# Starting the moving operands of the gate products 32 bytes past a multiple of 64

## The chip, the cores and the metric

The kernel runs on one core of a Trainium2 chip. The metric is the device time of one execution in microseconds (us): the median of three runs before the change is 1782.2 us (1781.26 to 1783.71). The engines are TensorE (PE; its loads of stationary operands are listed apart, as PEld), VectorE (DVE), ScalarE (ACT), GpSimd (POOL) and SyncE (SP), which issues nearly all DMAs. A matmul on PE takes a stationary operand, loaded first by its own LDWEIGHTS instruction, and a moving operand, which streams past it. Both are read from on-chip memory, where a tensor starts at the same byte address in each of 128 partitions. This document is about that address modulo 64.

## What is computed

64 graphs of 256 nodes with 256 features pass through two layers, each with a residual:

```
# layer 0
h = relu(layernorm(x));  x = x + relu(norm_adj @ h @ W.T + b)
# layer 1
h = relu(layernorm(x))
x_conv = relu(bn(conv17(relu(bn(conv1(h))))) + h)        # "branch"
A      = exp(-dist(h)) * adj;  msg = relu(h @ w_msg.T + b_msg)
x_nmp  = A @ msg                                        # "messages"
gi = concat(x_conv, x_nmp) @ w_ih.T + b_ih              # 512 -> 768
gh = h @ w_hh.T + b_hh                                  # 256 -> 768
r, z = sigmoid(gi_r + gh_r), sigmoid(gi_z + gh_z)
n = tanh(gi_n + r * gh_n)
x = x + (1 - z) * n + z * h
```

## The kernel before

**Products in three parts.** Most products are done on fp32r operands. Each fp32 tensor is split into a rounded high part and the remainder (names ending in h and l), and `mm3` (L99) yields for each block of 128 input features three matmuls: high by high, high by low, low by high. `multiply` (L109) issues them, so that all have line L111 in the profile, and are told apart by their operands: the profile writes `P<-moving,stationary` in no fixed order.

**Three stages.** The first (turns of one graph each) does layer 0 and the front of layer 1. Each turn has, on PE and in this order, 12 matmuls of 256 columns for layer 0 (`w0` moving, `ag` stationary), 12 of 256 columns for the messages (`ax` moving, `ms` stationary), 8 records of plain fp32 matmuls (`ah` moving, `hd` stationary), 2 for distances, 6 of 256 columns for the small projection (`xx` moving, `wse` stationary), 8 for a Fourier transform, 12 of 512 columns (`w1m` moving, `xx` stationary) and 4 transposes. The second stage multiplies spectra by filters, one frequency after another (`wh` moving, `xh` stationary, 256 columns). The third computes the gates, for 32 pairs of graphs, two output halves each.

**The third stage.** `gate` (L1056) takes its stationary operands from `wg` (128 columns of the weights w_ih and w_hh) and its moving operands from three tensors: `xcx` (branch, blocks 0 and 1), `nmx` (messages, blocks 2 and 3) and `xnx` (normalized input, blocks 4 and 5). Each is a high and a low tensor of 2 x 512 values per partition, and there are two of each for alternate pairs. A pair needs 18 blocks in each of two output halves, so 2 x 18 x 3 = 108 matmuls of 512 columns. In the very last half-pair the last 18 matmuls are split in two halves of 256 columns. Between the two halves of a pair 40 small matmuls of the inverse transform stand (`gt` moving, `yt` stationary, L1016). ACT writes the high parts (L979, L991, L1050), POOL and DVE the low parts (L986, L998, L1039). ACT and DVE evaluate the gates from PSUM, and DVE transposes and adds the result.

**Order of the work.** Each engine has its own program, written out by hand, and they wait for each other on semaphores. Nothing of the order depends on addresses.

**Addresses.** A `Place` (L72) hands out addresses in sequence and rounds each tensor's size up to a multiple of 32 bytes. `keep` starts at a multiple of 64 (L151). Which tensors start at 32 modulo 64 follows from the sizes (bytes per partition):

- `cold` (96 bytes) brings `gt` and `tt_w` to 32; `tt_w` (2268, rounded to 2272) brings all that follows back to 0.
- In the first stage `half`, `guard` (32 each) and `s2t` (148, rounded to 160) bring `sm`, `ag`, `xn`, `xt` and `xx` to 32 (L183 to L188); L190 starts again at a multiple of 64.
- `w0`, `w1m`, `wse`, `hd`, `ah`, `ax`, `ms`, `wh`, `xh`, `xsum`, `wsum` and `wg` start at 0.
- `xnx`, `nmx` and `xcx`, the third stage's moving operands, start at 0.

All these offsets within a tensor (blocks of 128, 256 or 512 values) are multiples of 64 bytes, so an operand has the same remainder as its tensor.

| matmuls | moving starts at | stationary starts at | columns |
|---|---|---|---|
| `w0`, `ag` (layer 0) | 0 | 32 | 256 |
| `ax`, `ms` (messages) | 0 | 0 | 256 |
| `xx`, `wse` (small projection) | 32 | 0 | 256 |
| `w1m`, `xx` (conv1 and msg) | 0 | 32 | 512 |
| `wh`, `xh` (frequencies) | 0 | 0 | 256 |
| gates | 0 | 0 | 512 |

Of the kernel before, what the change touches and what calls it, by code (L numbers as in the profile page):

```python
# [126 lines left out]
def gnn_kernel(nc, x, adj, adjt, w0t, w1mt, wset, wgt, w2r, bc, cols, ftab, gtab, ttab, eye, out):  # L127
# [19 lines left out]
    with ExitStack() as ctx:  # L147
# [13 lines left out]
        third = Place(nc, keep.at)  # L161
# [3 lines left out]
        third = Place(nc, keep.at)  # L165
        wf = [keep("wf0", [128, 20, 2, 256])]
        raw_wg = [third(f"st_wg{c}", [128, 768]) for c in range(6)]
        xnf = [third(f"xnf{i}", [128, 2, 2, 256]) for i in range(2)]
        nms = [third(f"nms{i}", [128, 2, 256]) for i in range(2)]
        xnx = [third.hl("xnx0", [128, 2, 512])]  # L170

        p1, p2, p3 = Place(nc, keep.at), Place(nc, keep.at), Place(nc, keep.at)
# [54 lines left out]
        mt = [p2(f"mt{i}", [128, 256]) for i in range(2)]  # L227
        yo = [p2(f"yo{i}", [128, 512]) for i in range(4)]

        xnx.append(p3.hl("xnx1", [128, 2, 512]))  # L230
        yt = [p3(f"yt{i}", [128, 5, 128]) for i in range(4)]
        nmx = [p3.hl(f"nmx{i}", [128, 2, 512]) for i in range(2)]
        xct = [p3(f"xct{i}", [128, 2, 256]) for i in range(2)]
        xcx = [p3.hl(f"xcx{i}", [128, 2, 2, 256]) for i in range(2)]
        oo = [p3(f"oo{i}", [128, 2, 2, 256]) for i in range(2)]
        tr = p3("tr", [128, 512])
        tz = p3("tz", [128, 512])
# [1316 lines left out]
```

## Time and profile before

| | |
|---|---|
| median of three runs | 1782.2 us |
| profiled execution, first to last instruction | 1779.4 us |
| PE busy | 1765.8 us, 99% |
| PEld, DVE, ACT, POOL busy | 87%, 68%, 56%, 47% |
| TensorE matmuls | 10778 |
| first stage | to about 655 us |
| second stage | to about 900 us |
| third stage | the rest, about 875 us |

No device time of the profiled execution is given apart from its span, 1779.4 us, which stands 2.8 us under the median of the runs. "Busy" of PE is the sum of the intervals in which at least one matmul is recorded; since a matmul of 512 columns is recorded with 390 ns and the next one starts some 227 ns later, the busy time and the mean duration do not tell the rate. The rate is read from the starts in the timeline: the difference of two starts by the number of matmuls between them.

### The profile page before, as it was taken

To read this page: it belongs to the slowest core of one execution; us is meant where nothing else is said; L and a number is where in the kernel's file an instruction comes from. 1 tells how busy PE (TensorE), PEld (TensorE's weight loads), DVE (VectorE), ACT (ScalarE), POOL (GpSimd) and SP (SyncE) were. 2 spreads that over 40 slices of the span, in tenths; PEclk is the share of its full clock that TensorE was granted. 3 is DMA by queue.
4 is the path that set the end of the run, shared out by engine and by line. 5 is a ranking of instruction groups with operands and counts; after the bars stand their busy time and mean duration, and the time that the engine had idled before them with its cause. 6 is when DMAs were issued, how large, how long until landed. Compare 5 with 4: busy or idle time off the path is not lost.

```text
span 1779.4 us, 30974 instructions
## 1 busy us (share of the span) xinstructions
PE 1765.8 (99%) x10778; PEld 1556.5 (87%) x10778; DVE 1211.7 (68%) x2318; ACT 1001.1 (56%) x1787; POOL 830.1 (47%) x988
## 2 busy tenths in 40 slices
PE   8999999999999999999999999999999999999998
PEld 7999999999999999999988888888888888888887
DVE  8999999999999946555664554554544545545545
ACT  6888888888888866656643233332333332333322
POOL 5788888887777627665722221221221222212211
PEclk9999999999999999999999999999999999999999
DMA  7566667666656464544663434435445344344342
GB/s 224 174 206 208 209 204 209 203 207 196 207 182 205 141 176 145 176 161 173 234 188 96 102 95 116 94 97 120 86 102 125 79 108 106 92 115 95 98 111 42
DMA packets 531865, 262.70 MB, mean 148 GB/s; under 512 B 366215, under 2 KB 494471, under 8 KB 531710
## 3 DMA queue, kind: packets, MB, share of 16 engines
q1 hardware_dynamic: 531166, 260.66, 52.5%
q8 instruction: 87, 1.43, 0.3%
q14 instruction: 68, 0.56, 0.1%
q10 hardware_dynamic: 544, 0.07, 0.0%
HBM read 151.58 MB, written 109.05 MB: 146 GB/s over the span
## 4 chain that ended last, share of the span: by engine, by line
PE 96%; DVE 1%; issue 1%; POOL 1%; ACT 0%; DMA 0%; DVEq 0%; POOLq 0%; ACTq 0%
PE P L111 72%; PE P L612 6%; PE P L1016 4%; PE P L871 4%; PE P L641 4%; PE P L703 4%; PE P L660 1%; PE P L621 1%; POOL axl L575 0%; POOL af L572 0%; DVE sm L483 0%; DVE sm L489 0%; DMA x<-in_x 0%; DVE agl L417 0%; DVE x L470 0%
## 5 line engine op out<-in xcount | busy, mean ns | idle before, releaser
L998 POOL TENSOR_TENSOR xnx1l<-xnf,xnx1h 128x1024 fp32r<-128x1024 f32 x16 | 43.9, 2744 | 343.7 <-ACT xnx1h L991 343.7
L998 POOL TENSOR_TENSOR xnx0l<-xnf,xnx0h 128x1024 fp32r<-128x1024 f32 x15 | 41.5, 2768 | 311.5 <-ACT xnx0h L991 311.5
L1117 ACT ACTIVATE tr<-P,cold 128x512 f32<-128x512 f32 x64 | 44.2, 690 | 213.1 <-PE P L111 213.1
L1120 ACT ACTIVATE nn<-gn,col 128x512 f32<-128x512 f32 x64 | 46.4, 724 | 183.0 <-DVE gn L1141 183.0
L1137 DVE SCALAR_TENSOR_TENSOR gn<-tr,gn 128x512 f32<-128x512 f32 x64 | 45.4, 709 | 138.8 <-ACT tr L1117 138.8
L572 POOL TENSOR_TENSOR af<-af,at 128x512 f32<-128x512 f32 x64 | 110.4, 1725 | 42.2 <-ACT af L363 40.3
L575 POOL TENSOR_TENSOR axl<-af,axh 128x512 fp32r<-128x512 f32 x64 | 101.3, 1582 | 55.6 <-ACT axh L381 55.6
L1150 DVE SCALAR_TENSOR_TENSOR tz<-tz,tr 128x512 f32<-128x512 f32 x63 | 43.6, 692 | 119.4 <-ACT tz L1131 119.4
L612 PE MATMUL P<-ah,hd 128*128 128x256 f32 x512 | 121.7, 381 | 0.3 <-ACT hd L397 0.3
L1131 ACT ACTIVATE tz<-P,cold 128x512 f32<-128x512 f32 x63 | 43.4, 688 | 133.7 <-PE P L111 133.7
L111 PE MATMUL P<-w1mh,xxh 128*128 128x512 f32 x256 | 107.8, 421 | 0.0
L1141 DVE TENSOR_TENSOR gn<-gn,P 128x512 f32<-128x512 f32 x64 | 44.0, 688 | 88.2 <-PE P L111 88.1
L612 PEld LDWEIGHTS P<-ah,hd 128*128 128x128 f32 x512 | 93.2, 191 | 10.7 <-ACT hd L397 0.5
L111 PE MATMUL P<-w1mh,xxl 128*128 128x512 f32 x256 | 101.3, 396 | 0.0
L111 PE MATMUL P<-w1ml,xxh 128*128 128x512 f32 x256 | 101.0, 395 | 0.0
L495 DVE SCALAR_TENSOR_TENSOR x<-x,x 128x512 f32<-128x512 f32 x64 | 99.6, 1557 | 0.1
L896 DVE TENSOR_TENSOR yo<-P,mt 128x512 f32<-128x512 f32 x78 | 53.5, 686 | 66.2 <-PE P L111 66.2
L1016 PEld LDWEIGHTS P<-gt,yt 64*128 64x128 f32 x1280 | 76.4, 187 | 11.3 <-issue 11.3
L111 PE MATMUL P<-w0h,agh 128*128 128x256 f32 x256 | 77.1, 301 | 4.3 <-DVE w0l L460 2.1
L1016 PE MATMUL P<-gt,yt 64*128 64x72 f32 (+2 forms) x1280 | 81.0, 278 | 0.0
L703 PE MATMUL P<-tt_w,taps 119*128 119x140 f32 (+1 forms) x592 | 80.8, 282 | 0.0
L723 ACT COPY wf<-P 128x420 f32<-128x420 f32 (+1 forms) x94 | 46.8, 512 | 60.0 <-PE P L703 59.8
(214 smaller groups left out, 6413.2 us busy)
## 6 DMA issues: line engine op xcount, KB each, us to landing
xh_d<-xst SPq DMA_DIRECT2D x64, 320.0 KB, 4.8
y_d<-yo SPq DMA_DIRECT2D x80, 256.0 KB, 2.1
yt<-y_d SPq DMA_DIRECT2D x128, 160.0 KB, 3.9
xl<-xh_d SPq DMA_DIRECT2D x36, 512.0 KB, 4.6
x<-in_x SPq DMA_DIRECT2D x64, 256.0 KB, 2.7
a<-in_adj SPq DMA_DIRECT2D x64, 256.0 KB, 3.0
at<-in_adjt SPq DMA_DIRECT2D x64, 256.0 KB, 4.1
x_d<-x SPq DMA_DIRECT2D x64, 256.0 KB, 4.4
```

The source lines that it names most:

```text
L111: done = e.matmul(o, l, r, start=start, stop=stop, skip_group_check=True)
L495: e.e.scalar_tensor_tensor(out=o[:, :, :], in0=o[:, :, :], scalar=0.0, in1=xs[b % 5][:, :, :], op0=ALU.max, op1=ALU.add).then_inc(S["x2"], 1)
L572: e.e.tensor_tensor(af[:, :], af[:, :], at[b % 7][:, :], ALU.mult).then_inc(S["am"], 1)
L575: e.e.tensor_tensor(ax[1][:, :], af[:, :], ax[0][:, :], ALU.subtract).then_inc(S["axlo"], 1)
L612: t = e.e.matmul(P[AG][:, f * 256:f * 256 + 256], hd[b % 2][:, m, f * 128:f * 128 + 128], ah[b % 2][:, m * 256:m * 256 + 256], start=m == ...
L641: t = e.e.matmul(P[k][:, n * 2 * NT:n * 2 * NT + 2 * NT], h1[b % 2][:, n, c * 128:c * 128 + 128], ft[:, :], start=True, stop=True, skip_gr ...
L703: t = e.e.matmul(P[k][:, m * 140:m * 140 + 140], taps[0:n_rows, j0 + m, c * 128:c * 128 + 128], tt_w[0:n_rows, part * 140:part * 140 + 140 ...
L723: e.e.copy(dst, src).then_inc(S["wev"], 1)
L871: t = e.e.matmul(common(chunk)[:, 0:256], xsum[f % 3][:, c, 128 * chunk:128 * chunk + 128], wsum[f % 3][:, c, :], start=c == 0, stop=c == ...
L896: e.e.tensor_tensor(yo[n % 4][:, :].rearrange("p (q o) -> p q o", q=2), main(chunk)[:, :].rearrange("p (q o) -> p q o", q=2), mt[chunk][:, ...
L998: e.e.tensor_tensor(o[1][:, :, :], xnf[p % 2][:, :, :, :].rearrange("p c i t -> p c (i t)"), o[0][:, :, :], ALU.subtract).then_inc(done, 1)
L1016: t = e.e.matmul(P[idft_bank(b, o)][:, first:end], y[rows, q, :], gt[rows, g:g + end - first], start=q == 0, stop=q == 4, skip_group_check ...
```

## The change

Two lines of padding of 32 bytes are put ahead of the moving operands, so that `xnx0`, `xnx1`, `nmx` and `xcx` start at 32 modulo 64. `nmx` and `xcx` now stand next to `xnx1`, and `yt`, `xct` and the rest come behind them, after a third padding that brings them back to 0 modulo 64. `xct`, `yt`, `oo`, `tr`, `tz`, `gn`, `nn`, `ot` and `x2l` have other addresses than before and the same remainder, 0. `wg` stays where it was. No instruction, no wait, no shape and no order on any engine changes.

```diff
@@ -167,6 +167,7 @@
         raw_wg = [third(f"st_wg{c}", [128, 768]) for c in range(6)]
         xnf = [third(f"xnf{i}", [128, 2, 2, 256]) for i in range(2)]
         nms = [third(f"nms{i}", [128, 2, 256]) for i in range(2)]
+        third.at += 32
         xnx = [third.hl("xnx0", [128, 2, 512])]
 
         p1, p2, p3 = Place(nc, keep.at), Place(nc, keep.at), Place(nc, keep.at)
@@ -227,11 +228,13 @@
         mt = [p2(f"mt{i}", [128, 256]) for i in range(2)]
         yo = [p2(f"yo{i}", [128, 512]) for i in range(4)]
 
+        p3.at += 32
         xnx.append(p3.hl("xnx1", [128, 2, 512]))
+        nmx = [p3.hl(f"nmx{i}", [128, 2, 512]) for i in range(2)]
+        xcx = [p3.hl(f"xcx{i}", [128, 2, 2, 256]) for i in range(2)]
+        p3.at += 32
         yt = [p3(f"yt{i}", [128, 5, 128]) for i in range(4)]
-        nmx = [p3.hl(f"nmx{i}", [128, 2, 512]) for i in range(2)]
         xct = [p3(f"xct{i}", [128, 2, 256]) for i in range(2)]
-        xcx = [p3.hl(f"xcx{i}", [128, 2, 2, 256]) for i in range(2)]
         oo = [p3(f"oo{i}", [128, 2, 2, 256]) for i in range(2)]
         tr = p3("tr", [128, 512])
         tz = p3("tz", [128, 512])
```

## Rows read from the trace of the kernel before

**Rows 1.** The page: span, busy time of engines, granted TensorE clock by slice.
```profile
span 1779.4 us, 30974 instructions
...
PE 1765.8 (99%) x10778; PEld 1556.5 (87%) x10778; DVE 1211.7 (68%) x2318; ACT 1001.1 (56%) x1787; POOL 830.1 (47%) x988
...
PEclk9999999999999999999999999999999999999999
```

**Rows 2.** Windows: the third stage; one pair of it. PE, PEld, DVE, ACT, POOL busy.
```profile
905.00:1779.40 874.40, 869.26 (x4753) 723.08 (x4751) 442.08 (x651) 282.71 (x418) 191.10 (x93) 1.00 0.44 101
1302.35:1329.52 27.17, 27.17 (x151) 22.58 (x149) 13.65 (x21) 8.83 (x14) 6.18 (x4) 1.00 0.45 102
```

**Rows 3.** Chain that ended last, in that pair: start us, us, what.
```profile
1302.42 24.70 PE P L111 x108
1327.12 2.46 PE P L1016 x40
```

**Rows 4.** Waits, PE, whole span: us in total, times, longest.
```profile
PE P L111 <- DVE w0l L460: 2.1, 1, 2.1
```

**Rows 5.** Waits, all engines, third stage.
```profile
ACT tr L1117 <- PE P L111: 213.1, 64, 3.4
```

**Rows 6.** Groups of gate matmuls by form: count, busy us, mean ns.
```profile
L111 PE MATMUL P<-xnx0h,wgh 128*128 128x512 f32 x192 | 76.5, 398 | 0.0
...
L111 PE MATMUL P<-xcx1l,wgh 128*128 128x512 f32 x190 | 73.9, 389 | 0.0
...
L111 PE MATMUL P<-xnx1l,wgh 128*128 128x256 f32 x4 | 1.1, 283 | 0.0
```

**Rows 7.** Timeline of PE, gates of one pair: start us, us, what.
```profile
1302.69 0.39 PE L111 MATMUL P<-xnx0l,wgh 128*128 128x512 f32 x1
...
1304.52 0.39 PE L111 MATMUL P<-xnx0h,wgh 128*128 128x512 f32 x1
...
1326.74 0.39 PE L111 MATMUL P<-xcx1h,wgl 128*128 128x512 f32 x1
```

**Rows 8.** Timeline of PE, first stage: conv1 and msg.
```profile
284.95 0.39 PE L111 MATMUL P<-w1ml,xxh 128*128 128x512 f32 x1
...
287.28 0.40 PE L111 MATMUL P<-w1mh,xxl 128*128 128x512 f32 x1
287.52 0.60 PE L660 MATMUL P<-ident,xn 128*128 128x128 f32 x4
```

**Rows 9.** Timeline of PE, same turn: layer 0, messages, fp32, small projection.
```profile
288.07 0.28 PE L111 MATMUL P<-w0l,agh 128*128 128x256 f32 x1
...
289.36 0.28 PE L111 MATMUL P<-axh,msh 128*128 128x256 f32 x1
...
289.71 0.28 PE L111 MATMUL P<-axh,msh 128*128 128x256 f32 x1
...
290.67 0.28 PE L111 MATMUL P<-axh,msl 128*128 128x256 f32 x1
290.79 1.89 PE L612 MATMUL P<-ah,hd 128*128 128x256 f32 x8
292.33 0.59 PE L621 MATMUL P<-uv 96*128 96x256 f32 x2
292.76 0.28 PE L111 MATMUL P<-xxh,wseh 128*128 128x256 f32 x1
...
293.46 1.25 PE L641 MATMUL P<-ft,h 128*128 128x160 f32 x8
```

**Rows 10.** Timeline of PE, last half gates, 256 columns.
```profile
1770.02 0.28 PE L111 MATMUL P<-xnx1h,wgl 128*128 128x256 f32 x1
...
1773.98 0.28 PE L111 MATMUL P<-xcx1h,wgl 128*128 128x256 f32 x1
```

**Rows 11.** ACT casts: tensors at 32 modulo 64; at 0.
```profile
L336 ACT CAST xxh<-xt 128x512 fp32r<-128x512 f32 x64 | 39.7, 620 | 3.8 <-DVE s2t L1391 1.8
L381 ACT CAST axh<-af 128x512 fp32r<-128x512 f32 x64 | 39.7, 620 | 2.6 <-POOL af L572 1.1
```

## The prediction

> **What bounds the kernel now.** I read the page's busy times first: PE is busy 1765.8 of 1779.4 us, and the granted clock is 9 tenths or more in each of the 40 slices, so full speed (2.4 GHz) nearly throughout [rows 1]. The windows then give the third stage, where the change lies: 874.40 us at a clock of 1.00, PE busy 869.26, the next engine, DVE, 442.08 [rows 2]. One pair of graphs takes 27.17 us, in which PE has no gap and DVE is busy 13.65, ACT 8.83, POOL 6.18 [rows 2]. The chain that ended last runs through PE alone there: 24.70 us of gate matmuls, 2.46 of the inverse transform [rows 3]. PE waits for nobody in this stage; its longest wait of the whole run is 2.1 us, at the start [rows 4]. The others wait for PE, as ACT's 213.1 us for the gate r [rows 5]. So in this stage time is the number of matmuls by the distance of their starts, and only that distance counts.
>
> The last view is the timeline, which gives it. In a pair the first matmuls start 228.8 ns apart (1302.69 to 1304.52 over 8), and then the distance settles: 1304.52 to 1326.74 over 98 is 226.7 ns, the same for all three tensors [rows 7]. At 2.4 GHz 512 columns stream in 213.3 ns (512 / 2.4), so each matmul pays 13.4 ns beyond its streaming. The change can only act on this piece, or add to it.
>
> **What the change does, step by step.** No instruction is added or moved, no wait either. Three things change: the remainder of the moving operands (0 to 32), of what ACT, DVE and POOL write when they fill them, and the plain position of some other tensors.
>
> *How many matmuls.* The three tensors times the three products give nine groups for the even pairs, with 192 matmuls of 512 columns each, and nine for the odd pairs, with 190 each: 9 x 192 + 9 x 190 = 3438. The last half-pair adds nine groups of 4 with 256 columns, 36 (the first, the last and a short one of these groups are shown) [rows 6].
>
> *What each costs at other remainders.* No matmul of the trace has 512 columns with the moving operand alone at 32, so I bound it by the nearest rows. The nearest in size is conv1 and msg: 512 columns, moving at 0, stationary at 32. Its starts lie 233.0 ns apart (284.95 to 287.28 over 10), or 233.6 with the step to the transposes (to 287.52 over 11) [rows 8]; I take 233.3. That is 6.6 ns over the gates' 226.7. It is not the busier first stage that makes it slow: messages, both operands at 0, run at 120.0 ns in the same turn (289.71 to 290.67 over 8) [rows 9], and the last half gates, both at 0 in the quiet third stage, at 120.0 ns too (1770.02 to 1773.98 over 33) [rows 10]. So a row with both at 0 runs alike in both stages, and what differs in conv1 is the remainder.
>
> Does a moving operand at 32 act like a stationary one at 32? With 256 columns the trace has both. Layer 0 (stationary at 32): 288.07 to 289.36 over 11, 117.3 ns. Small projection (moving at 32): 292.76 to 293.46 over 6, 116.7 ns. Both at 0: 120.0 [rows 9]. The two mixed cases agree within the rounding of the rows and differ from the equal case by the same 3 ns. I read this as: what counts is whether the two streams have the same remainder. Equal ones settle in a fixed rhythm (226.7, 120.0), unequal ones don't. With 256 columns that is a little faster, since there the load of the stationary operand is nearly as long as the matmul; with 512 it is slower. By this the gates go from 226.7 to 233.3 ns.
>
> *The sum.* 3438 x 6.6 ns = 22.7 us. The first 8 of each pair already stand at 228.8, so they lose 2.1 less: 32 x 8 x 2.1 ns = 0.5 us off. The 36 short ones may gain 36 x 3 ns = 0.1. Net +22.1 us. Made against the profiled span: 1779.4 + 22.1 = 1801.5; the runs' median stands 2.8 over the span, so 1804.3. I forecast 1804 us.
>
> *Bounds of this term.* From above: single steps in conv1, such as 287.28 to 287.52, are 240 ns by the rows [rows 8]; 3438 x 13.3 = +46 us. From below: the plain fp32 matmuls, whose moving operand is used at half the rate, start at most 220 ns apart (290.79 to 292.33 holds at least 7 steps) [rows 9], and nothing excludes that a broken rhythm lets the gates reach it: 3438 x (220 - 226.7) = -23 us. I take the value of the row nearest in columns, which is conv1's.
>
> *The writes.* ACT's cast between tensors at 32 takes 620 ns, and the same cast between tensors at 0 takes 620 ns [rows 11]: nothing on ACT. Were DVE's or POOL's low parts slower, the cover is large: DVE is idle 13.5 of a pair's 27.17 us, and POOL 21 [rows 2]. Cost 0; without that cover it would be a few hundred ns per pair.
>
> *The moved tensors.* `yt`, the stationary operand of the inverse transform, keeps its remainder, as do all of DVE's and ACT's work tensors. Only distances between addresses change; I know of no row in which distance shows. Cost 0, with the 0.2% band as its bound.
>
> *A rule that speaks against this.* The Trainium skill, "TensorE: Matmul & The Clock Gate", section "Part 2: What happens when you issue a matmul", says that PE has two independent read ports and that loading the next stationary operand takes no bandwidth from the running matmul; its section "Back-to-back issue gap" gives N/2.4 + 2.5 ns, 215.8 for 512 columns. The trace doesn't agree: 226.7 with both operands at 0, and 233 in conv1. "SBUF — State Buffer", section "Specifications (TRN2)", names lines of 16 bytes; both 0 and 32 are whole lines, and its section "Operand start alignment" makes address a matter of legality. By these pages the sum would be 0, which is the first rival below.
>
> **The rivals.**
>
> *No effect (1782).* The moving stream's start doesn't matter, and conv1 is slow because its stationary operand begins at 32 (a load that touches one more piece of 64 bytes). For it: conv1's odd side is indeed the stationary one, and the gates' stays at 0. Against it: the small projection, with only the moving side at 32, leaves 120.0 ns just as layer 0 does. The time would be 1782.2.
>
> *Faster.* The fixed rhythm of equal remainders is itself the loss. With unequal ones the load's reads fall between the moving stream's, and each matmul saves what it saves with 256 columns. The place is the start of each gate matmul, the price 120.0 - 117.0 = 3 ns, 3438 x 3 = 10.3 us: 1772. If it reached the fp32 matmuls' 220 ns, 1759. It decides as soon as the step falls under 225.7 ns (3.6 us, 0.2% of the time, by 3438 is 1 ns). Against it: conv1 has unequal remainders at 512 columns and is slower than the gates, and there the saving would have to appear as well.
>
> *Slower by another amount.* The moving stream touches 33 pieces of 64 bytes instead of 32. If it pays just for the two halves, half of conv1's excess or up to double of it are both possible: 3.3 ns, 1793, or 13.3 ns, 1828.
>
> *The change doesn't do what it says.* All sizes ahead of the padding are multiples of 64 but for those listed, so each of the twelve moving tensors does land at 32. I give this no chance of its own.
>
> **Chances.** Conv1's rate, 1804, with its own range 1798 to 1811: 0.52. Slower by another amount: 0.15 (two thirds of it below 1798). No effect: 0.18. Faster: 0.15. The band within which a measurement of this kernel can't tell a change is about 0.2%, 3.6 us. The slower side has 0.67; a little of the no-effect case and of the smallest losses falls across the band's edge, so slower 0.68, same 0.17, faster 0.15. The range that holds the time 8 times in 10 takes in no effect, the half excess and conv1's rate: 1779 to 1813.
>
> **What would show it.** In the timeline of the changed kernel the starts of a pair's gate matmuls would lie 233 ns apart and never settle at 226.7; the pair's period would go from 27.17 to about 27.87 us, the chain's piece of 108 from 24.70 to about 25.4, the third stage from 874.4 to 896.5. The first two stages would stay within 1 us, the 40 matmuls of the inverse transform at 2.46 us, PE without waits in the stage. It would be wrong if the steps stayed at 226.7 (the stationary side alone counts), if they fell below it (the rhythm was the loss), or if the time came from another place, such as a wait of PE on DVE or POOL.

## The result, and the profile after

The changed kernel takes 1803.15 us (median of 4 runs, 1802.9 to 1803.56), the kernel before 1781.73 us beside it. The ratio is 1.012 (95% interval 1.0108 to 1.0132), so it is 21.4 us slower. The forecast was 1804.

The windows of the changed kernel (one pair of graphs, then the third stage; columns as in [rows 2]):

```profile
1312.80:1340.67 27.87, 27.87 (x151) 22.56 (x149) 13.68 (x21) 8.84 (x14) 6.20 (x4) 1.00 0.47 99
905.00:1801.80 896.80, 891.53 (x4756) 722.55 (x4754) 442.70 (x651) 282.89 (x418) 191.41 (x93) 1.00 0.45 98
```

Against [rows 2], the pair went from 27.17 to 27.87 us and the stage from 874.40 to 896.80, with the busy times of DVE, ACT and POOL within 1 us of before, and the same clock. The chain through that pair:

```profile
1310.42 2.46 PE P L1019 x40
1312.89 25.39 PE P L111 x108
```

Against [rows 3], 108 gate matmuls take 25.39 instead of 24.70 us; the 40 of the inverse transform still take 2.46. The timeline of PE in the same pair, 1 and 95 matmuls apart, shows the step:

```profile
1315.72 0.40 PE L111 MATMUL P<-nmx0h,wgh 128*128 128x512 f32 x1
1315.95 0.39 PE L111 MATMUL P<-nmx0l,wgh 128*128 128x512 f32 x1
...
1337.88 0.39 PE L111 MATMUL P<-xcx1h,wgl 128*128 128x512 f32 x1
```

1315.72 to 1337.88 over 95 is 233.3 ns, where [rows 7] have 226.7. The duration of one, 0.39 or 0.40, shows almost nothing of it. The last half gates, 256 columns:

```profile
1792.29 0.28 PE L111 MATMUL P<-xnx1l,wgh 128*128 128x256 f32 x1
...
1796.26 0.28 PE L111 MATMUL P<-xcx1h,wgl 128*128 128x256 f32 x1
```

1792.29 to 1796.26 over 34 is 116.8 ns, where [rows 10] have 120.0: the short matmuls became faster, as the short rows of the first stage had suggested. Who fills the moving operands is not slower; ACT's cast of the normalized input, before and after:

```profile
L991 ACT CAST xnx0h<-xnf 128x1024 fp32r<-128x1024 f32 x16 | 16.6, 1036 | 0.0
```

```profile
L994 ACT CAST xnx0h<-xnf 128x1024 fp32r<-128x1024 f32 x16 | 16.6, 1036 | 0.0
```

### The profile page after: what moved, and what is told of

Its sections match the earlier page's. It is cut to its first block, busy times and chain, and to the rows that moved or that the text cites. A ratio compares the mean times of both kernels' runs of the same rounds, so it can differ in the third digit from the quotient of the medians.

```text
span 1801.8 us, 30974 instructions
## 1 busy us (share of the span) xinstructions
PE 1786.6 (99%) x10778; PEld 1554.7 (86%) x10778; DVE 1212.7 (67%) x2318; ACT 1001.2 (56%) x1787; POOL 830.0 (46%) x988
## 4 chain that ended last, share of the span: by engine, by line
PE 96%; issue 1%; DVE 1%; POOL 1%; DMA 0%; ACT 0%; SPq 0%; DVEq 0%; POOLq 0%; ACTq 0%
PE P L111 73%; PE P L615 6%; PE P L1019 4%; PE P L874 4%; PE P L644 4%; PE P L706 4%; PE P L663 1%; PE P L624 1%; PE P L1478 0%; DMA tt_w<-in_ttab 0%; POOL axl L578 0%; POOL af L575 0%; DVE sm L486 0%; DVE sm L492 0%; DVE x L473 0%
## 5 line engine op out<-in xcount | busy, mean ns | idle before, releaser
L874 PE MATMUL P<-wsum,xsum 128*128 128x256 f32 x312 | 80.2, 378 | 0.0
```

The costliest lines, as they stand in the source:

```text
L874: t = e.e.matmul(common(chunk)[:, 0:256], xsum[f % 3][:, c, 128 * chunk:128 * chunk + 128], wsum[f % 3][:, c, :], start=c == 0, stop=c == ...
```

## The experiments

Theory R, behind the forecast: what counts is whether the two operands of a matmul have the same remainder. Theory M: the moving operand's own start counts. "Distance" below is the start of the moving operand minus that of the stationary one, modulo 256. In each run I read the chain's piece of 108 gate matmuls (24.70 us before, 25.39 after). e1, e2, e3 and e10 were executed 4 to 11 times, the others once each; the kernel before took 1781.03 to 1783.71 us throughout.

**Padding of 64 instead of 32** (e1)

```diff
-        third.at += 32
+        third.at += 64
         xnx = [third.hl("xnx0", [128, 2, 512])]
-        p3.at += 32
+        p3.at += 64
         xnx.append(p3.hl("xnx1", [128, 2, 512]))
...                             # the third padding too: 64 for 32
```

> The changed kernel with paddings of 64 bytes instead of 32: the same new order of the tensors, but the moving operands of the gates start at 0 modulo 64 again. Theory R (what counts is whether the moving and the stationary operand of a matmul have the same remainder modulo 64): the gate matmuls start 226.7 ns apart, time as before, about 1782 us. Theory M (a moving operand must start at a multiple of 64, whatever the stationary one does): the same, 1782. Rival P (the new order or neighbours of the tensors cost, or the remainder that counts is modulo 128): 233.3 ns, about 1803 us.

```profile
1305.78 24.94 PE P L111 x108
```

Ratio to before 1.0043 (1.0028 to 1.0058): 1789.2 us. All starts are multiples of 64, and still 108 matmuls take 0.24 us more, 2.2 ns each. Neither theory had this, and the remainder modulo 64 is not the whole rule. The rival's time (1803) was wrong too, its kind (a longer remainder) right.

**Both operands at 32** (e2) and **the stationary one alone** (e3)

```diff
# e2: on the changed kernel; e3: on the kernel before
+        third.at += 32
         wg = third.hl("wg", [128, 6, 768])
```

> The changed kernel with 32 bytes of padding ahead of wg as well, so that the stationary and the moving operands of the gates both start at 32 modulo 64. Theory R (equal remainders): 226.7 ns from start to start, about 1782 us. Theory M (the moving operand's own start): 233.3 ns, 1803 us. A third, L (each operand that begins off a multiple of 64 costs by itself): more than 233.3 ns, up to 240, 1803 to 1826 us.

> The kernel before with 32 bytes of padding ahead of wg alone: stationary operands of the gates at 32 modulo 64, moving ones at 0, as in conv1 and msg of the first stage. Theory R: 233.3 ns, about 1803 us. Theory M: 226.7 ns, 1782 us, and then conv1's slow rate has another cause. Theory L: 233.3 ns, about 1803 us.

The chain of e2, then of e3:

```profile
1303.36 24.70 PE P L111 x108
```

```profile
1312.61 25.40 PE P L111 x108
```

e2 is at 1781.8 us, ratio 1.0001 (0.9991 to 1.0011); e3 at 1803.2, ratio 1.0121 (1.0106 to 1.0136). This decides between R and M: the change is undone by shifting the stationary operand as well, and done as fully by shifting it alone. Theory L falls with M, since in e2 both operands start off a multiple of 64 and nothing is lost. e2 has the new order of the tensors and all other new addresses, so these cost nothing.

**Only xnx at 32** (e4)

```diff
         xnx.append(p3.hl("xnx1", [128, 2, 512]))
+        p3.at += 32
         nmx = [p3.hl(f"nmx{i}", [128, 2, 512]) for i in range(2)]
         xcx = [p3.hl(f"xcx{i}", [128, 2, 2, 256]) for i in range(2)]
-        p3.at += 32
         yt = [p3(f"yt{i}", [128, 5, 128]) for i in range(4)]
```

> The changed kernel with nmx and xcx at multiples of 64 again, and xnx alone at 32. If the loss is paid matmul by matmul, the 36 of a pair's 108 that read xnx start 233 ns apart and the others settle at 226.7, and the span is about 36/108 of 22.4 = 7.5 us over 1779.4. If one odd group upsets the rhythm of the rest, the others stay at 230 or more, and the span is 15 us or more over.

```profile
1308.36 25.08 PE P L111 x108
```

The span is 1791.8 us, 12.4 over before, between the two expectations, which had overlooked that `nmx` and `xcx` land at a distance of 64 here, not 0. With e1's 2.2 ns for these, 36 x 6.6 + 72 x 2.2 ns = 0.40 us over 24.70; measured 0.38. So the loss is paid matmul by matmul, by each one's own distance, and the payments add up to within 0.02 us.

**Distances of 16 and 144 mixed, 96, 128, 256 and 512** (e5, e6, e7, e12, e13). In e5 each moving tensor is a view that begins 4 values into a tensor 32 values longer, on the kernel before. The 32 values are 128 bytes, so the high tensors, which come first, start at a distance of 16, and the low ones behind them at 144: of 108 matmuls 72 are at 16 and 36 at 144. The others are e1 with another number.

```diff
+    def hl16(self, name, shape):
+        n = math.prod(shape[1:])
+        flat = [self(f"{name}{h}", [128, n + 32], F32R)[:, 4:4 + n] for h in "hl"]
...
-        third.at += 32
+        third.at += 96      # e6; e7: 128, e12: 256, e13: 512; p3.at the same
```

> The kernel before with the moving operands of the gates starting 16 bytes into slightly longer tensors: 16 modulo 128, stationary ones at 0. So far the step from start to start is 226.7 ns at a difference of 0, 229.0 at 64 and 233.3 at 32 (all modulo 128). Theory R in its narrow form (the same 64-byte piece is what counts, each stream a whole number of pieces apart): anything off 0 is as bad as 32, 233 ns, a span of about 1801 us. Rival G (the step depends on the distance in a graded way): between 226.7 and 233.3, a span of 1780 to 1800.

> The changed kernel with paddings of 96 bytes: moving operands at 96 modulo 128, stationary at 0. The run with wg alone moved had the difference -32, the same as 96 modulo 128, and 233.3 ns. Theory R (only the difference counts): 233.3 ns, and the span within 1 us of 1801.6. If the absolute start of the moving operand matters beside the difference: another step, and a span at least 3 us away.

> The changed kernel with paddings of 128 bytes, the control for the run with 64, which lost 7.7 us where neither theory expected a loss. If the remainder modulo 128 is what counts: 226.7 ns, span about 1779.4 us. If the order or the neighbours of the tensors cost: 229 ns as with 64, span about 1787 us. If still larger distances count (256 or 512): something else than 226.7.

> The changed kernel with paddings of 256 bytes. At a distance of 128 between the two operands' remainders the step was 232.7 ns and not the 226.7 that theory R expected, so the remainder modulo 64 is too short a rule. Theory R512 (the moving and the stationary start must agree modulo 512 bytes, the length of one stationary row of 128 values, which is the remainder that all gate operands share in the kernel before and in the run with both at 32): at 256 no fixed step, 229 to 234 ns, a span of 1787 to 1803 us. Theory R256 (agreement modulo 256 is enough): 226.7 ns, a span of 1780 us.

> The changed kernel with paddings of 512 bytes, otherwise as the one with 256. Both R512 and R256: 226.7 ns, span 1779.4 to 1780.5 us. Rival Q (still larger distances count, or the padding itself): 229 to 234 ns, span 1787 to 1803 us.

The chain's piece of one pair in each of the five, in this order, and behind that of e5 four starts in a row:

```profile
1310.03 25.16 PE P L118 x108
...
1311.46 0.40 PE L118 MATMUL P<-xnx0h,wgh 128*128 128x512 f32 x1
1311.70 0.40 PE L118 MATMUL P<-xnx0l,wgh 128*128 128x512 f32 x1
1311.93 0.39 PE L118 MATMUL P<-xnx0h,wgl 128*128 128x512 f32 x1
1312.15 0.40 PE L118 MATMUL P<-xnx0h,wgh 128*128 128x512 f32 x1
```

```profile
1313.07 25.40 PE P L111 x108
```

```profile
1311.48 25.30 PE P L111 x108
```

```profile
1303.35 24.71 PE P L111 x108
```

```profile
1303.38 24.71 PE P L111 x108
```

The last half gates of the same runs give the step of matmuls of 256 columns, from the second start to the 36th. That of e6, as an example:

```profile
1792.58 0.28 PE L111 MATMUL P<-xnx1l,wgh 128*128 128x256 f32 x1
...
1796.66 0.27 PE L111 MATMUL P<-xcx1h,wgl 128*128 128x256 f32 x1
```

| distance | 0 | 16 and 144 (e5) | 32 | 64 | 96 | 128 | 224 (e3) | 256 | 512 |
|---|---|---|---|---|---|---|---|---|---|
| 108 matmuls of 512 columns, us | 24.70 | 25.16 | 25.39 | 24.94 | 25.40 | 25.30 | 25.40 | 24.71 | 24.71 |
| step at 256 columns, ns | 120.0 | 117.9 | 116.8 | 117.6 | 120.0 | 118.5 | 117.9 | 120.0 | 120.0 |

First the row of 512 columns. e5 lies within rival G's range and below the narrow theory's 233 ns, but it shows the mean of two distances: in the rows the step to and from a low tensor is 0.24 and 0.23 us and the one between two high tensors 0.22, again and again. What 16 alone costs is not shown. At 96 the loss is the same as at 224 (e3), as the theory of the difference said, though by a rule modulo 128 that then failed: at 128 the loss is nearly full (every third pair takes 25.40 us, the others 25.29 or 25.30), and at 256 it is gone. R512 was too strict, R256 held: of the distances tried, all multiples of 256 run at the fast step and no other does. Distances of 160 and 192 were not tried at 512 columns.

The row of 256 columns, of 34 steps each, is not the first one turned round. All multiples of 256 are at 120.0 here too, but 96 is as well, although it costs the long matmuls as much as any; 32 gains 3.2 ns and 224, its mirror image, only 2.1.

**Half the load** (e8 on the kernel before, e9 on the changed one)

```diff
-            w = [{c: h[:, c, n * 256 + o * 128:n * 256 + o * 128 + 128] ...
+            w = [{c: h[:, c, n * 256 + o * 128:n * 256 + o * 128 + 64] ...
-            return multiply(e.e, mm3(w, mov, P[k][:, 0:end - at], ...
+            return multiply(e.e, mm3(w, mov, P[k][0:64, 0:end - at], ...
```

> The kernel before, but each gate matmul takes 64 of its 128 stationary columns and writes 64 partitions of its result; the other half of the gates is left out, all other work stays. Moving columns and their number are unchanged. Theory R explains the 13.4 ns that a gate matmul takes beyond the 213.3 ns of its streaming by reads of the stationary operand that collide with the moving stream's: half as many reads, so 6 to 8 ns beyond, a step of 219 to 222 ns, and a span 16 to 26 us below 1779.4. Rival S (the 13.4 ns are a fixed price of starting an fp32r matmul): 226.7 ns, span as before.

> The changed kernel (moving operands of the gates 32 bytes off the stationary ones), with 64 of 128 stationary columns in each gate matmul; half of the gates is left out, all other work stays. With half the load and no distance the short matmuls had gone from 120.0 to 113.3 ns, but the long ones from 226.7 to 229.8, without a fixed rhythm. Theory C (what a matmul takes beyond its streaming are collisions of the two read streams, in proportion to the load): beyond 213.3 ns half of 20, so about 223 ns, and short ones at about 112 ns; a span near 1767 us. Rival W (with a short load no distance settles, and 229 to 230 ns is what any unsettled long stream takes): 229 to 230 ns, a span near 1788 us, the same as at no distance. If the distance costs by itself whatever the load: 233 ns, span 1801.

The chain of e8, and from its timeline two starts of short matmuls:

```profile
1306.50 24.98 PE P L111 x108
```

```profile
1778.98 0.28 PE L111 MATMUL P<-xnx1h,wgl 128*64 128x256 f32 x1
...
1782.72 0.28 PE L111 MATMUL P<-xcx1h,wgl 128*64 128x256 f32 x1
```

The same of e9:

```profile
1308.74 25.08 PE P L111 x108
```

```profile
1782.90 0.28 PE L111 MATMUL P<-xnx1h,wgh 128*64 128x256 f32 x1
...
1786.71 0.28 PE L111 MATMUL P<-xcx1h,wgl 128*64 128x256 f32 x1
```

With half the load and distance 0 the short matmuls fall from 120.0 to 113.3 ns (3.74 us over 33): what they take beyond 106.7 ns halves (106.7 ns is what 256 more columns add at distance 0, 226.7 - 120.0, and so an estimate of the streaming of 256). But the long ones get slower, 24.98 instead of 24.70 us. At distance 32 the long ones gain (25.08 instead of 25.39) and the short ones, from 1782.90 over 32 steps, are at 119.1 ns, slower than with the full load. A fixed price per matmul (rival S) is out, and so is a price in proportion to the load (theory C). The edit also halves the partitions of the result that a matmul writes, so by itself it doesn't say that the load is what counts; that the stationary operand's address counts is shown by e3. Of rival W half came: its step was nearly right, about 230 ns in e8 and 231 in e9, but not "the same as at no distance", since e9's span is 1792.2 us and e8's 1788.1.

**A version with distances chosen** (e10)

```diff
+        p1.at += 96
         w1m = p1.hl("w1m", [128, 2, 512])
+        p1.at += 32
...
+        p1.at += 32
         ax = p1.hl("ax", [128, 512])
+        p1.at += 96
...
+        p2.at += 32
         wh = [p2.hl(f"wh{i}", [128, 2, 2, 256]) for i in range(3)]
+        p2.at += 96
```

> The kernel before with three shifts. (1) w1m moved by 96 bytes and all behind it by 128, so that w1m and xx, the operands of conv1 and msg (512 columns), have the same remainder modulo 512: the step there goes from 233.3 towards 226.7 ns; by the gates' 12 first, which take some rounds to settle, 4 us over 64 turns. (2) ax moved by 32 against ms and (3) wh by 32 against xh, matmuls of 256 columns: the step goes from 120.0 to about 116.7 ns as in the last half gates of the changed kernel; 64 x 11 x 3.3 ns = 2.3 us and 80 x 9 x 3 ns = 2.2 us. Theory R512 with its reverse for 256 columns: sum -8.5 us, about 1773 us. Rival D: in the first stage VectorE, busy 567 of 586 us, has become the bound, so that (1) and (2) give less than half: 1776 to 1779 us. If the distance mattered only in the gates: 1781.5.

The chain of the kernel before at conv1 in two turns five apart, at the first frequency and at the first gates; then of e10:

```profile
560.21 2.80 PE P L111 x12
...
609.38 2.80 PE P L111 x12
...
672.35 1.66 PE P L111 x12
...
903.19 8.31 PE P L111 x42
```

```profile
559.30 2.74 PE P L111 x12
...
608.26 2.74 PE P L111 x12
...
670.95 1.65 PE P L111 x12
...
899.98 8.32 PE P L111 x42
```

1777.46 us against 1781.54, ratio 0.9977 (0.9968 to 0.9986): 4.1 us less than the kernel before, where 8.5 were expected. The second stage gives 1.8 us (230.84 to 229.03), of 2.2 expected. In the first stage conv1's 12 take 2.74 instead of 2.80 us, but a turn only falls from 9.834 to 9.792 us, 0.04, where the two shifts should have saved 0.10 (0.06, and 11 x 3.3 ns). The trace says where the rest stays. VectorE's low part of layer 0's stationary operand (`agl`), the last transposes and the first load of layer 0, in a turn of the kernel before and in one of e10:

```profile
572.22 0.68 DVE L417 TENSOR_TENSOR agl<-P,agh 128x512 fp32r<-128x512 f32 x1
572.68 0.60 PE L660 MATMUL P<-ident,xn 128*128 128x128 f32 x4
573.01 0.19 PEld L111 LDWEIGHTS P<-w0h,agh 128*128 128x128 f32 x1
```

```profile
571.30 0.68 DVE L423 TENSOR_TENSOR agl<-P,agh 128x512 fp32r<-128x512 f32 x1
571.63 0.60 PE L666 MATMUL P<-ident,xn 128*128 128x128 f32 x4
572.04 0.19 PEld L111 LDWEIGHTS P<-w0h,agh 128*128 128x128 f32 x1
```

Before, the load starts 0.33 us behind the first transpose in every turn, and 0.12 to 0.13 behind the end of `agl`. In e10 it starts at varying times behind the transposes (0.41 us here), and 0.07 us behind the end of `agl` in 47 of the 51 turns between 100 and 600 us: PE has caught up with VectorE and waits for it, some 0.03 us a turn. That is rival D. Another 0.01 us goes to layer 0, whose distance became 160 by the way: 118.2 ns a step instead of 117.3.

## Why the prediction was right

**What bounds the stage.** As read: PE without waits, the other engines' busy times unchanged, and the loss in the start-to-start step. The view of PE's waits is empty for the third stage after the change, as it was before it.

**How many, and what each costs.** 3438 x 6.6 ns, 22.1 net, was forecast; the span grew by 22.4 us (1779.4 to 1801.8) and the runs by 21.4. In the span 21.9 of it lie in the third stage, counted from its first gates (at 903.19 us before, at 903.73 after); the other 0.5 lies ahead of it and is within the scatter of the runs of the kernel before. The step of 233.3 ns taken from conv1 came out to the tenth. There is a reason: `w1m` starts at 97024 and `xx` at 120544 bytes past `keep`, a distance of -23520, which is 32 modulo 256, exactly the gates' new one. The prediction compared them modulo 64 only, so that they also agree modulo 256 was luck. It was luck that mattered little: a remainder of 32 modulo 64 can be 32, 96, 160 or 224 modulo 256, and three of these were measured, at 25.39 to 25.40 us.

**The step from the span to the runs.** The forecast added 2.8 us to the span, the distance of the median of three runs from the profiled span. In the runs recorded with a span of their own the time stands 1.75 to 1.88 us over it (1803.56 and 1801.8 for the changed kernel), so about 1 us of the 2.8 was scatter between runs. With 1.8 the same sum gives 1803.3, against 1803.15 measured.

**Does a moving operand at 32 act like a stationary one at 32?** With 512 columns yes, by e2 and e3: the difference counts, and 32 costs the same in either direction. With 256 columns, where the prediction read it, not quite. Its two mixed cases are not alike modulo 256: layer 0 is at a distance of 32, the small projection at 224. That both gain "the same 3 ns" came from few rows and their rounding; in the last half gates 32 gains 3.2 ns and 224 gains 2.1.

**What was too short.** "The same remainder" was meant modulo 64, after the allocator's unit and the table of starts. The range and the time didn't depend on it, since 32 is off by either rule. But with the same reasoning I would have called paddings of 64 and 128 free, and they cost 7.7 us and about 20 (span 1799.3). "Equal remainders settle in a fixed rhythm" is right only modulo 256. The gain at 256 columns came in the gates as well (116.8 after).

**The writes and the moved tensors.** 0, as forecast: 1036 ns for the cast as before, and e2 at before's time with every new address. But the reason given, that no row shows a distance between addresses to matter, was wrong: conv1's rows show just that. The zero held all the same. The moved stationary operand `yt` belongs to small plain fp32 matmuls; its distance from `gt` went from 96 to 32 modulo 256 (224 in e1, 160 in e6), and the 40 matmuls take 2.46 us in all of them. Whether fp32r matmuls of that size would have paid wasn't tested.

**The two read ports.** The Trainium skill, "TensorE: Matmul & The Clock Gate", section "Part 2: What happens when you issue a matmul", has the two read ports of TensorE as independent, so that a load takes nothing from the running matmul. Here shifting the loaded operand alone by 32 bytes costs 21.7 us (e3). For these fp32r matmuls the measurement decides against it.

**What stays open.** Why 256, why a short matmul can gain where a long one loses, and why it doesn't at 96. The runs show a fixed step of 226.7 or 120.0 ns at distances that are multiples of 256; at the others tried 512 columns take about 229 to 233 ns and 256 columns 116.8 to 120.0. The mechanism behind was only argued (reads of the two streams that meet in a steady or a changing order), not shown.

## What to carry to other kernels

In an fp32r stream bound by TensorE, look at the difference of the start addresses of moving and stationary operand modulo 256: 0 for matmuls of 512 columns; for those of 256, 32 was the best of the distances tried, and 96 gained nothing. The plain fp32 matmuls of the inverse transform showed no difference. Read the step from start to start in the timeline, not the duration of a matmul, and compare steps of like shapes within one kernel: the kernel's own slow rows are the best price for a layout. Padding ahead of one tensor shifts all behind it, so check the distance of every pair, not only of the one that was meant (here e4, e5 and e10 each had a distance that wasn't intended). And a faster stream can run into the next engine: of the 6.3 us expected of e10's first stage 1.4 came by the starts of the second stage (672.35 and 670.95), or 2.7 by 64 turns of 0.042.

## What was not expected of the hardware

- The address of an operand changes a matmul's rate by up to 3% (226.7 to 233.3 ns) at an unchanged instruction, clock and shape. At 64 bytes it is 1% (24.94 for 24.70 us), at 128 it is 2.4% (25.30).
- The same distance that slows 512 columns speeds up 256 columns by 2.7% (120.0 to 116.8 ns); a distance of 96 slows the long ones as much and leaves the short ones at 120.0.
- A smaller stationary operand can make matmuls slower: with 64 instead of 128 of its columns, and half the partitions of the result, 24.98 us for 24.70.
